# Moving the next chunk's row statistics and row scales to the start of a chunk

## Time and profile before

| | us |
|---|---|
| median of 3 runs | 1353.34 |
| lowest to highest | 1353.05 to 1354.01 |
| profiled execution | 1353.88 |
| its span (first to last instruction) | 1352.1 |
| TensorE busy | 1231.7 (91%) |
| VectorE busy | 1117.3 (83%) |
| ScalarE busy | 1068.6 (79%) |
| GpSimd busy | 378.2 (28%) |

### The profile page before, as it was taken

One profiled execution on the slowest core, in us unless ns is written; L12 is line 12 of the kernel. 1 busy time (PEld: TensorE's weight loads), 2 busy tenths in 40 slices (PEclk: granted clock), 3 DMA queues, 4 the chain that ended last, 5 costly groups with the idle time before them and its releaser, 6 DMA issues.

```text
span 1352.1 us, 19064 instructions
## 1 busy us (share of the span) xinstructions
PE 1231.7 (91%) x6144; PEld 634.3 (47%) x6144; DVE 1117.3 (83%) x1894; ACT 1068.6 (79%) x1885; POOL 378.2 (28%) x465
## 2 busy tenths in 40 slices
PE   0279999999999999999999999999999999999995
PEld 0134454545545454544545454454545454454542
DVE  5978888888888888888888878888797888889784
ACT  0448879888787988878798888879888887988885
POOL 4115241231414123141413213141321404132211
PEclk8589999999999999999999999999999999999997
DMA  9201021120302112030211203021120302110011
GB/s 324 54 2 32 1 56 40 33 62 3 92 1 61 34 39 56 5 90 0 62 33 44 51 14 81 1 63 31 44 51 16 80 0 64 31 47 17 16 48 32
DMA packets 38836, 61.21 MB, mean 45 GB/s; under 512 B 9552, under 2 KB 9808, under 8 KB 38736
## 3 DMA queue, kind: packets, MB, share of 16 engines
q1 hardware_dynamic: 38448, 59.87, 17.1%
q10 hardware_dynamic: 288, 0.08, 0.0%
HBM read 43.14 MB, written 16.78 MB: 44 GB/s over the span
## 4 chain that ended last, share of the span: by engine, by line
PE 67%; POOL 9%; DVE 9%; ACT 8%; issue 6%; DMA 1%; SPq 0%; DVEq 0%; POOLq 0%
PE blk L423 25%; PE blk L440 22%; PE side L384 9%; PE side L408 4%; ACT blk L527 3%; DVE blk L635 3%; ACT y_full L520 2%; DVE g_lo L612 2%; PE side L372 2%; POOL out_sb L949 1%; POOL out_sb L952 1%; PE side L361 1%; POOL row_z L911 1%; POOL v L915 1%; POOL v L916 1%
## 5 line engine op out<-in xcount | busy, mean ns | idle before, releaser
L527 ACT ACTIVATE blk<-blk,ratio 128x512 f32<-128x512 f32 x960 | 623.9, 668 | 114.2 <-PE blk L440 109.2
L635 DVE TENSOR_SCALAR blk<-blk,ratio 128x512 f32<-128x512 f32 x768 | 576.2, 752 | 157.2 <-PE blk L423 149.8
L423 PE MATMUL blk<-h_hi,q_sb 128*128 128x512 f16 x1024 | 391.9, 383 | 81.0 <-DVE blk L635 42.5
L423 PE MATMUL blk<-h_lo,q_sb 128*128 128x512 f16 x1024 | 391.1, 382 | 0.0
L440 PE MATMUL blk<-y_hi,w_sb 128*128 128x512 f16 x1024 | 389.4, 380 | 0.0
L440 PE MATMUL blk<-y_lo,w_sb 128*128 128x512 f16 x1024 | 389.1, 380 | 0.0
L646 DVE SCALAR_TENSOR_TENSOR y_lo<-y_full,up,y_hi 128x512 f16<-128x512 f32 x256 | 231.5, 904 | 0.0
L949 POOL TENSOR_TENSOR out_sb<-fin,s_rows 128x512 f32<-128x512 f32 x62 | 79.2, 1278 | 505.5 <-ACT fin L539 502.3
L520 ACT ACTIVATE y_full<-blk,par,last 128x512 f32<-128x512 f32 x256 | 199.6, 780 | 16.0 <-PE blk L423 14.7
L423 PEld LDWEIGHTS blk<-h_hi,q_sb 128*128 128x128 f16 x1024 | 100.2, 98 | 216.2 <-DVE blk L635 92.8
L934 POOL TENSOR_TENSOR h_lo<-h_full,h_hi 128x512 f16<-128x512 f32 x64 | 94.2, 1472 | 364.4 <-DVE h_hi L619 350.2
(11 more groups left out here) (132 smaller groups left out, 1159.0 us busy)
## 6 DMA issues: line engine op xcount, KB each, us to landing
xt<-in_x SPq DMA_DIRECT2D x64, 256.0 KB, 4.7
x_again<-in_x SPq DMA_DIRECT2D x256, 64.0 KB, 1.9
out<-out_sb SPq DMA_DIRECT2D x256, 64.0 KB, 1.7
w_sb<-in_q SPq DMA_DIRECT2D x4, 1024.0 KB, 13.8
zt<-in_q SPq DMA_DIRECT2D x2, 1024.0 KB, 15.3
y_hi<-in_q SPq DMA_DIRECT2D x1, 1024.0 KB, 10.7
y_lo<-in_q SPq DMA_DIRECT2D x1, 1024.0 KB, 13.0
s_rows<-in_wqkv SPq DMA_DIRECT2D x1, 768.0 KB, 8.5
```

The source lines that it names most:

```text
L423: mm = pe.matmul(blk[J % 2][:], q1_sb[:, g, j // 4, w, j % 4 * P:(j % 4 + 1) * P], a[:, c % 2, g, :], start=(g == 0 and n == 0), stop=(g = ...
L527: act.activation(blk2[hb][:], blk2[hb][:], ACT.Copy, scale=ratio2[:, KC * j + hb:KC * j + hb + 1]).then_inc(blk2_scaled, 1)
L635: dve.tensor_scalar(blk[J % 2][:], blk[J % 2][:], ratio1[:, at:at + 1], None, ALU.mult).then_inc(blk_scaled, 1)
```

## The change

One line of the slot table changes: the four statistics go from slots 16, 17, 20, 24 to 0, 1, 2, 3, the moments from 25 and 27 to 5 and 6, and GpSimd's rows with its row scales from 30 to 8. The normalise slots stay. No instruction is added or removed, and the streams of TensorE, ScalarE and SyncE stay as they are.

```
--- before.py
+++ after.py
@@ -36,7 +36,7 @@
 TILE_AT, JOB_AT = (0, 12, 24, 36), (0, 3, 5, 8, 10)
 TURN_AT = (43, 48, 54, 59)
 TURN_Z_AT = (18, 21, 25, 28)
-STATS_AT, MOMENTS_AT, ROWS_AT, NORMALISE_AT = (16, 17, 20, 24), (25, 27), 30, (33, 34, 37, 40)
+STATS_AT, MOMENTS_AT, ROWS_AT, NORMALISE_AT = (0, 1, 2, 3), (5, 6), 8, (33, 34, 37, 40)
 FIN_LAG, OUT_LAG = 2, 3
 TURN_LAG, HHIGH_LAG, HLOW_LAG, READ_LAG = 2, 3, 4, 1
```

## The result

| | before | after |
|---|---|---|
| median of 4 runs, us | 1353.19 | 1333.04 |
| lowest to highest | 1351.77 to 1354.01 | 1332.36 to 1333.29 |
| span of the profiled execution | 1352.1 | 1331.5 |

The ratio is 0.9851, 95% interval 0.9834 to 0.9868: 20.2 us faster. The forecast was 1337.7, 15.6 us faster, with 1327 to 1347 as the range.

What follows compares the result with a forecast made beforehand. TensorE's own work was taken as the bound, its idle gaps behind GpSimd's rows as winnable. Per chunk 1.62 + 0.16 - 0.65 = 1.13 us, 14 times 15.8, less 0.25: 15.6 us won, 1337.7 us, range 1327 to 1347.

Steps and rivals of the forecast that it cites:

- Term 1: Slots 31 to 36, chunks 1 to 14: without rows in between, slot 36 starts 1.62 us earlier per chunk.
- rival A: Slot 31: the output moved forward doesn't hold y_hi up; 8.1 us more won, 1329.6 us; chance 0.15.
- Term 2: Slots 0 to 7, chunks 1 to 14: added statistics delay rescales before slots 6 and 7; 0.65 us lost per chunk.
- B: Slots 4 to 7 cost nothing: 9.1 us more won, 1328.6 us; chance 0.11.
- E: Slots 0 to 7: backlog passed on whole, 2.72 us on TensorE per chunk; 13.4 us slower, 1366.8; chance 0.05.
- Term 3: Slots 16 to 27, relieved of statistics: wo of slot 22 follows sooner; 0.16 us won per chunk.
- Term 4: Chunk 0: statistics behind the reductions lose 2.40 us, the removed gap wins 2.15; net 0.25 us lost.
- C: Both places, slots 31 to 36 and 0 to 7, cost more: 8.4 us more, 1346.1 us; chance 0.11.
- D: The removed wait for GpSimd's rows is replaced by one of the same length: 1353 us; chance 0.05.

Runs made afterwards that it cites:

- e3: Changed kernel with GpSimd's fourth output of a chunk made to wait until slot 34's normalise is done: 1323.63 us, 0.9782 of the kernel before.
- e2: Changed kernel with one of four BN_STATS moved from slot 3 to 8, moments to 9 and 10, rows to 11: 1324.13 us, 0.9781 of the kernel before.
- e1: Changed kernel with GpSimd's rows put back from slot 8 to slot 30, statistics and moments left moved: 1362.46 us, 1.0065 of the kernel before.
- e4: Changed kernel with the old slots for statistics, moments and rows in chunk 0 only: 1334.45 us, 0.986 of the kernel before.

## Why the prediction came out right, and 4.6 us short

**Term 1, slots 31 to 36** (1.62 forecast): slot 36 is 1.62 us earlier than before, counted from slot 32 (46.08 - 40.26 = 5.82, before 47.30 - 39.86 = 7.44). The mechanism was right in its parts: y_hi ended 0.27 us after L949's end (0.28 forecast), the normalise found GpSimd's output gone by, and e3 shows that the hold-up is the output, since without it y_hi takes 0.47 us and the 0.65 us come back. The Trainium skill's rule of the exclusive lock (SBUF — State Buffer, Who interferes with whom) is borne out in both directions, by y_hi here and by GpSimd's 1.66 us in e3; rival A is out.

**Term 2, slots 4 to 7** (0.65 forecast): 0.64 to 0.65 measured, at the two slots named, 0.45 of it at slot 6 (0.46 forecast). e2 shows that it hangs on the last statistic, e1 that it is there without GpSimd's move. Rivals B and E are out: the backlog is neither free nor handed on whole, but counts from where a rescale misses its date.

**Term 3, slot 22** (0.16 forecast, at most 0.3): 0.26 (slot 23 is 0.39 us late against 0.65 before it). The row of wo at 257.14 is two matmuls merged, and I took only the delay of the first. 14 x 0.10 = 1.4 us.

**Term 4, chunk 0** (0.25 lost forecast): the part of it that was costed held: the matmul that was at 69.98 starts at 72.49, of which 0.15 are from the preparation, so about 2.4. (The prediction calls it slot 4's; it is slot 6's, since ffn1 has no step in slots 1 and 3 of chunk 0.) But by the chunk's end 1.6 us are won. The step that failed is "the gap of 2.15 us is won": behind this gap TensorE ran at half its clock for 3.4 us, and that cost 1.7 us more, which e4 brings back; the wait itself was worth 2.3 us, not the bracket's 2.15. The same fall of the clock came behind one of the 14 later gaps in each trace of the kernel before (80.09 - 78.40 = 1.7 us). The two falls are 3.4 us of the 5.0 by which the spans' difference was under-forecast; term 3 is 1.4 more, and the wait in chunk 0 most of the rest. The evidence was there to read: the matmuls behind the gap at 114.76 start 0.42 us apart, where they are 0.22 apart elsewhere, and the page's row of granted clocks hides it, since a slice there is the mean of 33.8 us and reads 9. I had priced a gap by its length alone. All these misses go the same way, so nothing in the forecast was right by their cancelling.

Rivals C and D did not come: nothing took the removed wait's place.

What stays open is why the clock falls after some gaps of 2.0 us and not after others of the same length. The four traces with such gaps (the kernel before twice, e1, and chunk 0 of e4) have 46 of them, and it fell after 8: in chunk 0 each of the four times, otherwise after 4 of 42, in changing chunks; the new gaps of 0.29 and 0.67 us were never followed by it. No run here shows what makes the difference.

## What to carry to other kernels

Where one engine hands work back to another every few slots, an instruction on it costs nothing until the hand-over misses its date, and then all of it: work out the date of each hand-over from the rows, and put extra work where the other engine's side jobs leave a pause, not where a table has room. Of a chain over three engines ask which part's move brings the gain; here that was GpSimd's rows, and the statistics, which have to stand before them, cost 0.65 us per chunk in slots 0 to 3 and nothing in slots 8 to 12. And when a queue gets shorter, ask what its later work now runs into: a large instruction on GpSimd that moves forward holds up VectorE's SBUF work.

## What the runs showed of the hardware

- A TensorE gap of 2.0 us costs more than its length on average: behind 8 of 46 such gaps the granted clock was at 1.2 GHz for about 3.4 us, which cost 1.7 us each.
- The hold-up between VectorE and GpSimd falls on whoever comes second, for the whole rest of the other's instruction: y_hi 1.12 us instead of 0.48 behind L949, L951 of the same work 1.66 instead of 1.27 behind y_lo. Rescales in PSUM (L635) were not touched: they took 0.74 to 0.76 us beside an output too. A small instruction of GpSimd's was: behind y_lo (268.48 to 269.98), the first of rows (128x4) took 0.64 us in slot 30 of the kernel before, and 0.20 in slot 8 of the changed one.

```profile
269.40 0.64 POOL L910 TENSOR_TENSOR v<-mv,row_const 128x4 f32<-128x4 f32 x1
```

```profile
236.63 0.20 POOL L910 TENSOR_TENSOR v<-mv,row_const 128x4 f32<-128x4 f32 x1 [8.55 <-DVE mv L601]
```
